# GNN hops: the weighted one-hot matrices of eight edge tiles are made by two VectorE instructions in place of eight

## The chip, the cores and the metric

The program runs on one core of one Trainium2 chip. The metric is the device time of one execution in microseconds (us), as the median of repeated runs. TensorE does the matrix products, VectorE and ScalarE elementwise work, GpSimd (POOL in the rows) issues the indexed gathers, SyncE plain DMAs. In rows PE is TensorE, PEld its weight loads, DVE is VectorE, ACT is ScalarE.

## The reference

Four layers follow one another on 6250 nodes with 256 features: a graph attention layer, a mixture of experts, a three-hop graph network, an LSTM that steps through the 6250 nodes. The change is in the third. There, with 100,000 edges:

```python
for i in range(3):
    msg = H[cols] * vals[:, None]
    Hn = jax.ops.segment_sum(msg, rows, num_segments=N)
    Hn = Hn @ Wn[i].T + bn[i]
    Hs = H @ Ws[i].T + bs[i]
    H = Hn + Hs
    if i != hop_num - 1:
        H = jax.nn.elu(H)
```

The kernel multiplies H by `Wn` first and puts the result into a table in DRAM (`hop_table`). What is left of a hop is: fetch one table row of 256 floats for each edge, scale it by the edge's weight, add it into the row of its target node. That is the function `propagate`.

## The kernel before

Edges are sorted by target and cut into tiles of 128, such that all targets of a tile lie in one block of 128 nodes. There are 832 tiles, padded ones at the end included. A hop takes them in rounds of U = 8, so 104 rounds, four rounds (NS = 4) to a loop body; three hops make 312 rounds and 2496 tiles. For a tile, a 128x128 matrix `S` has in row e the weight of edge e at the column of its target and zeros elsewhere; `S` transposed times the gathered rows `G` gives the sums of the tile, and these are added into block b of `agg` (in the last hop into `X`).

Each engine has a list of its own; semaphores alone tie them:

- **ScalarE** writes into a ring of four slots the row numbers of a round (`idx`, line 633; it waits until the gathers that used the slot four rounds ago have landed) and its targets and weights (`lw`, line 638).
- **GpSimd** issues eight indirect DMAs a round (line 657), 128 rows of 1 KB each, into slot r of `G`. It waits for `indexed`, and for `mm`: the products of four rounds earlier must be done.
- **TensorE** waits for the landing of the round's eight gathers (`got[r]`), then for each tile for `built` and `added`, and multiplies (line 671). Each float32 product is two MATMUL instructions in the trace.
- **VectorE** does two things in turn: `build` makes the `S` of one tile of the next round (line 680: compare `cols` with the tile's targets, times the weight), then the sum of one tile of this round is added (line 694: one operand from PSUM, one from SBUF) after a wait for that product. At the start of a round it loads eight block numbers (`TENSOR_LOAD`, line 608). `S` has two halves, used in turn.

A hop begins and ends with a barrier of all engines; between hops `hop_transform` makes the next table.

## Time and profile before

| | us |
|---|---|
| median of 3 runs | 17562.97 |
| lowest, highest | 17558.74, 17570.36 |
| span of the profiled execution | 17545.4 |
| a hop (4620 to 5685, 5798 to 6861, 6984 to 8048) | 1063 to 1065 each |
| the LSTM and what follows, from 8048 | 9497 |

The span is what the profiler sees of one execution on the core. A row of the timeline tells when an instruction, or a run of like ones, began, how long it took, and in brackets how long its engine had been idle before and what ended that. In grouped rows the number after the bar is the total busy time, then the mean of one in ns, then the idle time before them with what ended it. "issue" means that nothing in the profile was waited for.

### The profile page before, as it was taken

The numbers are of one execution on the slowest core, as the hardware profiler recorded it, in microseconds if no ns is written. First come the engines' busy times: TensorE is split into PE (matmuls) and PEld (weight loads), VectorE is DVE, ScalarE is ACT, GpSimd is POOL, SyncE is SP. The second block draws the span as 40 slices with busy tenths as digits, with TensorE's granted clock in tenths as the row PEclk, the third lists the DMA queues.
The fourth block names the chain that finished last, engine by engine and source line by source line (L and its number), as shares of the span: only waits on it lengthen the run. The fifth ranks groups of instructions, "written<-read, shape, count | busy, mean of one in ns | idle before, by whom it ended". The sixth has DMA issues, their size and how long they took to land. (4 is left out here: it accounts for less than half of the span.)

```text
span 17545.4 us, 683245 instructions
## 1 busy us (share of the span) xinstructions
PE 12730.7 (73%) x250869; PEld 10213.3 (58%) x250870; DVE 11697.3 (67%) x68713; ACT 5986.8 (34%) x41949; POOL 5631.1 (32%) x6174
## 2 busy tenths in 40 slices
PE   5247773399655656556888888888888888888887
PEld 3135552266444544445777777777777777777776
DVE  7368887322555454556777777777777777777777
ACT  0004442011100101003555555554555555555555
POOL 4778887666576575772000000000000000000000
PEclk6558886599877777775555555555555555555555
DMA  0102222111333333331000000000000000000000
GB/s 22 25 21 73 74 72 43 56 34 33 101 105 98 96 105 87 105 105 37 4 4 4 4 4 4 4 4 4 4 4 4 4 4 4 4 4 4 4 4 18
DMA packets 352412, 609.44 MB, mean 35 GB/s; under 512 B 157501, under 2 KB 232222, under 8 KB 348988
## 3 DMA queue, kind: packets, MB, share of 16 engines
q0 software_dynamic: 223104, 471.33, 10.4%
q1 hardware_dynamic: 126524, 100.27, 1.9%
q8 instruction: 1835, 30.06, 0.7%
q14 instruction: 949, 7.77, 0.1%
HBM read 508.72 MB, written 62.45 MB: 33 GB/s over the span
## 5 line engine op out<-in xcount | busy, mean ns | idle before, releaser
L2402 PE MATMUL lr_ZI<-ls_h,ls_V 128*128 128x1 f16 x150000 | 5006.8, 166 | 1669.7 <-DVE ls_h L2451 1412.8
L2402 PEld LDWEIGHTS lr_ZI<-ls_h,ls_V 128*128 128x128 f16 x150000 | 4487.3, 104 | 2677.0 <-DVE ls_h L2451 2640.4
L2419 ACT ACTIVATE ls_tg<-lr_ZI 128x2 f32<-128x2 f32 x12500 | 2150.0, 172 | 4626.5 <-PE lr_ZI L2402 4534.6
L2446 DVE TENSOR_TENSOR_SCAN lr_c<-ls_tg,ls_one_hc 128x2 f32<-128x2 f32 x12500 | 2118.1, 170 | 1441.0 <-ACT ls_tg L2419 1317.8
L2358 POOL COPY ls_HT<-ls_h 128x250 f32 x50 | 19.8, 395 | 9358.3 <-DVE ls_h L2456 9358.3
L2402 PE MATMUL lr_ZO<-ls_h,ls_V 128*128 128x1 f16 x75000 | 2865.0, 165 | 0.0
L671 PE MATMUL prop_sum<-prop_G,prop_S 128*128 128x256 f32 x4992 | 1830.4, 546 | 1369.9 <-DMA prop_G<-hop_table,prop_idx 1369.9
L657 POOL DMA_INDIRECT prop_G<-hop_table,prop_idx x2496 | 2368.3, 949 | 1057.3 <-issue 708.8
L2402 PEld LDWEIGHTS lr_ZO<-ls_h,ls_V 128*128 128x128 f16 x75000 | 2483.2, 104 | 0.0
L671 PEld LDWEIGHTS prop_sum<-prop_G,prop_S 128*128 128x128 f32 x4992 | 1403.9, 288 | 1796.3 <-issue 1486.1
L2451 DVE TENSOR_TENSOR ls_h<-ls_to 128x1 f16<-128x1 f32 x12500 | 2023.4, 162 | 479.1 <-ACT ls_to L2424 16.0
L2424 ACT ACTIVATE ls_to<-lr_c 128x1 f32<-128x1 f32 x12500 | 2102.5, 169 | 9.9 <-DVE lr_c L2446 1.0
L2422 ACT ACTIVATE ls_to<-lr_ZO 128x1 f32<-128x1 f32 x12500 | 2069.3, 171 | 0.0
L2455 DVE TENSOR_TENSOR_SCAN ls_h<-ls_to,ls_h 128x2 f16<-128x2 f32 x12500 | 1633.5, 162 | 25.7 <-issue 25.7
L694 DVE TENSOR_TENSOR gnn_agg<-gnn_agg,prop_sum 128x256 f32 x1664 | 694.9, 418 | 908.7 <-PE prop_sum L671 884.9
L2458 DVE TENSOR_TENSOR ls_one_hc<-ls_h,lr_c 128x1 f32<-128x1 f32 x6250 | 969.0, 155 | 220.0
L633 ACT CAST prop_idx<-gnn_SRT 128x8 int32 (+1 forms) x312 | 63.3, 203 | 2915.2 <-DMA prop_G<-hop_table,prop_idx 2903.7
L680 DVE TENSOR_SCALAR prop_S<-all_cols,prop_lw 128x128 f32<-128x128 f32 x2520 | 900.5, 358 | 165.6 <-issue 153.3
L2456 DVE TENSOR_TENSOR ls_h<-ls_to 128x2 f32<-128x2 f32 x6250 | 952.9, 152 | 7.2 <-issue 7.2
L2459 DVE TENSOR_TENSOR ls_one_hc<-ls_h,lr_c 128x1 f32<-128x1 f32 x6250 | 930.2, 149 | 0.0
L522 POOL DMA_INDIRECT sd_records<-sc_rec,sc_place x784 | 772.5, 985 | 440.7 <-issue 408.0
L1007 POOL DMA_INDIRECT all_X<-gat_table,gs_idx x832 | 825.3, 992 | 239.1 <-issue 239.1
(455 smaller groups left out, 13965.7 us busy)
## 6 DMA issues: line engine op xcount, KB each, us to landing
prop_G<-hop_table,prop_idx POOLq DMA_INDIRECT x2496, 2.7
mow_W<-in_L_ffn_W SPq DMA_DIRECT2D x16, 1024.0 KB, 10.8
moe_out<-me_Ys SPq DMA_DIRECT2D x108, 128.0 KB, 1.7
all_X<-gat_table,gs_idx POOLq DMA_INDIRECT x832, 2.8
hop_table<-ht_T SPq DMA_DIRECT2D x50, 256.0 KB, 2.1
sd_records<-sc_rec,sc_place POOLq DMA_INDIRECT x784
ss_records<-me_recs,me_places POOLq DMA_INDIRECT x540
gat_table<-gt_hs SPq DMA_DIRECT2D x50, 128.0 KB, 1.8
```

Of the source, the lines that this page charges most:

```text
L657: nc.gpsimd.indirect_dma_start(out=G[:, r, u, :], out_offset=None, in_=table[:, :], in_offset=bass.IndirectOffsetOnAxis(ap=idx[:, r, u:u + ...
L671: nc.tensor.matmul(ps[u][:, 0:D], S[:, r % 2, u, :], G[:, r, u, :], start=True, stop=True).then_inc(mm, 1)
L2402: mm = nc.tensor.matmul(place(hf, bank, col, 1), (V2 if part == "21" else V1)[:, q, ROWS.index(row), :], hx[:, prev, q, 1:2], start=False, ...
L2419: nc.scalar.activation(tg[:, s % 2, m, :], place(hf, m, col, 2), ACT.Tanh, scale=back).then_inc(gates[m], 1)
L2422: nc.scalar.activation(to[:, s % 2, m, 1:2], place(hf, KD + m, col, 1), ACT.Sigmoid, scale=back)
L2424: nc.scalar.activation(to[:, s % 2, m, 0:1], c[m][:, 1:2], ACT.Tanh, scale=0.5).then_inc(tanh_made[m], 1)
L2446: nc.vector.tensor_tensor_scan(c[m][:, 0:2], tg[:, e, m, :], one_hc[:, m, :], 1.0, ALU.mult, ALU.add).then_inc(cell[m], 1)
L2451: nc.vector.tensor_tensor(h1[:, r, m, 1:2], to[:, e, m, 1:2], to[:, e, m, 0:1], ALU.mult).then_inc(h1_made[m], 1)
L2455: nc.vector.tensor_tensor_scan(h2[:, r, m, :], to[:, e, m, :], h1[:, r, m, :], 1.0, ALU.mult, ALU.subtract).then_inc(h2_made[m], 1)
L2456: nc.vector.tensor_tensor(h[:, r, :], to[:, e, :, 1], to[:, e, :, 0], ALU.mult).then_inc(h_made, 1)
L2458: nc.vector.tensor_tensor(one_hc[:, 0, 1:2], h[:, r, 0:1], c[0][:, 1:2], ALU.mult)
L2459: nc.vector.tensor_tensor(one_hc[:, 1, 1:2], h[:, r, 1:2], c[1][:, 1:2], ALU.mult).then_inc(hc_made, 1)
```

## The change

`build` now makes all eight matrices of the next round at once with two instructions on 128x1024 elements. The first compares `cols`, repeated eight times, with `local`, each value repeated 128 times, and writes `same`; these three are bf16 tiles. The second multiplies `same` by `weight`, each value repeated 128 times, into the float32 half of `S`. Both have two operands in SBUF. The second waits for the first, and the first for the second of the round before (`compared` and program order). `build(n + 1)` stands behind the eight additions of round n; it stood between them tile by tile.

TensorE waits for `built` once a round, ahead of its first product. VectorE waits for `mm` ahead of every second addition, for two products at a time; it still waits for the addition before (`added`) each time. ScalarE makes `local` and `weight` by two copies in place of one. A bf16 copy of `cols` is made once a hop.

```diff
                 def prep(n, r, first=False):
                     if not first:
-                        act.wait_ge(built, U * (n - NS + 1))
-                    nc.scalar.copy(lw[:, r], SRT[:, bass.ds(n * U, U), 1:3]).then_inc(prepped, 1)
+                        act.wait_ge(built, n - NS + 1)
+                    nc.scalar.copy(local[:, r], SRT[:, bass.ds(n * U, U), 1])
+                    nc.scalar.copy(weight[:, r], SRT[:, bass.ds(n * U, U), 2]).then_inc(prepped, 1)
...
                         pe.wait_ge(got[r], before + i * (16 * U) + 16 * U)
+                        pe.wait_ge(built, n + 1)
                         for u in range(U):
-                            pe.wait_ge(built, n * U + u + 1)
                             pe.wait_ge(added, n * U + u + 1)
...
-                def build(n, r, u):
-                    if u == 0:
-                        dve.wait_ge(prepped, n + 1)
-                    nc.vector.tensor_scalar(S[:, r % 2, u, :], k.cols[:], lw[:, r, u, 0:1], lw[:, r, u, 1:2],
-                                            ALU.is_equal, ALU.mult).then_inc(built, 1)
-
-                for u in range(U):
-                    build(0, 0, u)
+                nc.vector.tensor_copy(cols[:], k.cols[:]).then_inc(compared, 1)
+
+                def build(n, r):
+                    dve.wait_ge(prepped, n + 1)
+                    dve.wait_ge(compared, n + 1)
+                    nc.vector.tensor_tensor(same[:], cols[:].unsqueeze(1).broadcast_to([P, U, P]),
+                                            local[:, r].unsqueeze(2).broadcast_to([P, U, P]), ALU.is_equal).then_inc(compared, 1)
+                    dve.wait_ge(compared, n + 2)
+                    nc.vector.tensor_tensor(S[:, r % 2], same[:], weight[:, r].unsqueeze(2).broadcast_to([P, U, P]),
+                                            ALU.mult).then_inc(built, 1)
+
+                build(0, 0)
                 with dve.Fori(0, QUADS) as i:
                     for r in range(NS):
                         n = NS * i + r
                         blocks = blocks_of(nc, mybir.EngineType.DVE, tile_block, n)
                         for u in range(U):
-                            build(n + 1, (r + 1) % NS, u)
                             b = blocks[u]
-                            dve.wait_ge(mm, NS * U + n * U + u + 1)
+                            if u % 2 == 0:
+                                dve.wait_ge(mm, NS * U + n * U + u + 2)
                             dve.wait_ge(added, U + n * U + u)
                             nc.vector.tensor_tensor(agg[:, bass.ds(b, 1), :], agg[:, bass.ds(b, 1), :],
                                                     ps[u][:, 0:D].unsqueeze(1), ALU.add).then_inc(added, 1)
+                        build(n + 1, (r + 1) % NS)
```

On VectorE, where one round of the first hop ends and the next begins, the kernel before has these rows (line, operation, output <- inputs, elements; `sum6` is the PSUM bank of tile 6):

```order
L694 TENSOR_TENSOR gnn_agg<-gnn_agg,prop0_sum6 128x256
L680 TENSOR_SCALAR prop0_S<-all_cols,prop0_lw 128x128
L692 REGISTER_ALU
L693 REGISTER_ALU
L694 ISA
L694 TENSOR_TENSOR gnn_agg<-gnn_agg,prop0_sum7 128x256
L608 ISA
L608 TENSOR_LOAD gnn_tbk
L679 REGISTER_ALU
L680 TENSOR_SCALAR prop0_S<-all_cols,prop0_lw 128x128
```

In this stretch one small instruction on `S` stands ahead of each addition.

On VectorE at the same place the changed kernel has:

```order
L700 TENSOR_TENSOR gnn_agg<-gnn_agg,prop0_sum6 128x256
L699 REGISTER_ALU
L700 ISA
L700 TENSOR_TENSOR gnn_agg<-gnn_agg,prop0_sum7 128x256
L684 TENSOR_TENSOR prop0_same<-prop0_cols,prop0_local 128x1024
L686 REGISTER_ALU
L687 TENSOR_TENSOR prop0_S<-prop0_same,prop0_weight 128x1024
L608 ISA
L608 TENSOR_LOAD gnn_tbk
L698 REGISTER_ALU
```

The additions now follow one another, and both large instructions stand between the last addition of a round and the load of the next block numbers.

## Rows read from the trace of the kernel before

**Rows 1.** Busy time by stage: one hop, and all behind the hops
```profile
core 0: us, PE busy (x) PEld busy (x) DVE busy (x) ACT busy (x) POOL busy (x), PEclk, DMA share, GB/s
...
4620.00:5685.00 1065.00, 610.69 (x1664) 468.19 (x1664) 559.10 (x1672) 38.16 (x210) 789.74 (x832) 0.73 0.38 102
...
8048.00:17545.00 9497.00, 7748.96 (x227648) 6678.26 (x227648) 7291.87 (x56538) 4782.49 (x37753) 20.86 (x54) 0.50 0.02 5
```

**Rows 2.** The page's costliest groups: the lines of the hops
```profile
L671 PE MATMUL prop_sum<-prop_G,prop_S 128*128 128x256 f32 x4992 | 1830.4, 546 | 1369.9 <-DMA prop_G<-hop_table,prop_idx 1369.9
L657 POOL DMA_INDIRECT prop_G<-hop_table,prop_idx x2496 | 2368.3, 949 | 1057.3 <-issue 708.8
...
L633 ACT CAST prop_idx<-gnn_SRT 128x8 int32 (+1 forms) x312 | 63.3, 203 | 2915.2 <-DMA prop_G<-hop_table,prop_idx 2903.7
L680 DVE TENSOR_SCALAR prop_S<-all_cols,prop_lw 128x128 f32<-128x128 f32 x2520 | 900.5, 358 | 165.6 <-issue 153.3
```

**Rows 3.** Line 657 alone: shortest, median and longest gather issue (ns)
```profile
L657 POOL DMA_INDIRECT prop_G<-hop_table,prop_idx x2496: 942/946/1032, 4622.2 to 8025.7; - x192
```

**Rows 4.** Timeline of a steady round, all engines
```profile
5503.58 0.95 POOL L657 DMA_INDIRECT prop_G<-hop_table,prop_idx  x1 [0.30 <-issue]
...
5504.83 0.94 POOL L657 DMA_INDIRECT prop_G<-hop_table,prop_idx  x1 [0.30 <-issue]
...
5506.60 5.38 PE L671 MATMUL prop_sum<-prop_G,prop_S 128*128 128x256 f32 x16 [4.67 <-DMA prop_G<-hop_table,prop_idx]
...
5507.90 0.42 DVE L694 TENSOR_TENSOR gnn_agg<-gnn_agg,prop_sum 128x256 f32 x1 [3.96 <-PE prop_sum L671]
5508.23 0.34 DVE L680 TENSOR_SCALAR prop_S<-all_cols,prop_lw 128x128 f32<-128x128 f32 x1
...
5508.75 0.42 DVE L694 TENSOR_TENSOR gnn_agg<-gnn_agg,prop_sum 128x256 f32 x1 [0.17 <-PE prop_sum L671]
...
5512.81 0.41 DVE L694 TENSOR_TENSOR gnn_agg<-gnn_agg,prop_sum 128x256 f32 x1
...
5516.58 5.38 PE L671 MATMUL prop_sum<-prop_G,prop_S 128*128 128x256 f32 x16 [4.61 <-DMA prop_G<-hop_table,prop_idx]
```

**Rows 5.** Timeline of the end of the first hop
```profile
5664.06 0.95 POOL L657 DMA_INDIRECT prop_G<-hop_table,prop_idx  x1 [0.30 <-issue]
...
5664.50 6.69 PE L671 MATMUL prop_sum<-prop_G,prop_S 128*128 128x256 f32 x16 [6.73 <-DMA prop_G<-hop_table,prop_idx]
...
5677.51 5.32 PE L671 MATMUL prop_sum<-prop_G,prop_S 128*128 128x256 f32 x16 [6.32 <-DMA prop_G<-hop_table,prop_idx]
...
5683.69 0.41 DVE L694 TENSOR_TENSOR gnn_agg<-gnn_agg,prop_sum 128x256 f32 x1
```

**Rows 6.** Groups of other VectorE instructions with two SBUF operands, by size
```profile
L1209 DVE TENSOR_TENSOR gs_M<-all_X,gs_M 128x512 f32<-128x512 f32 x208 | 142.1, 685 | 0.0
...
L247 DVE TENSOR_TENSOR sd_oh<-sdb_bins,sd_binrow 128x400 bf16<-128x400 f32 x138 | 77.6, 574 | 33.7 <-DVE sd_pos L343 27.1 <-PE sd_cnt L306 4.4 <-PEq L251 2.0
...
L1321 DVE TENSOR_TENSOR all_X<-all_X,gf_XL 128x12800 f32<-128x12800 f32 x1 | 13.5, 13493 | 0.0
```

**Rows 7.** Timeline of the first sort: GpSimd's DMA issues beside VectorE
```profile
299.65 0.57 DVE L339 TENSOR_TENSOR sd_ranks<-sd_rank,sd_run 128x400 f32<-128x400 f32 x1
...
299.98 0.96 POOL L522 DMA_INDIRECT sd_records<-sc_rec,sc_place  x1 [0.30 <-issue]
...
303.55 0.57 DVE L247 TENSOR_TENSOR sd_oh<-sdb_bins,sd_binrow 128x400 bf16<-128x400 f32 x1
303.76 1.20 POOL L522 DMA_INDIRECT sd_records<-sc_rec,sc_place  x1 [0.30 <-issue]
...
306.32 0.58 DVE L247 TENSOR_TENSOR sd_oh<-sdb_bins,sd_binrow 128x400 bf16<-128x400 f32 x1 [0.17 <-DVE sd_pos L343]
306.52 1.20 POOL L522 DMA_INDIRECT sd_records<-sc_rec,sc_place  x1 [0.31 <-issue]
```

**Rows 8.** Timeline in the first hop: a gather issue beside line 680
```profile
5519.68 0.34 DVE L680 TENSOR_SCALAR prop_S<-all_cols,prop_lw 128x128 f32<-128x128 f32 x1
5519.84 0.99 POOL L657 DMA_INDIRECT prop_G<-hop_table,prop_idx  x1 [0.30 <-issue]
```

More of the change, by code:

```diff
@@ L618, in propagate @@
         idx = ph.sb("idx", [P, NS, U], I32)
-        lw = ph.sb("lw", [P, NS, U, 2])
-        S = ph.sb("S", [P, 2, U, P])
+        cols = ph.sb("cols", [P, P], BF16)
+        local, weight = ph.sb("local", [P, NS, U], BF16), ph.sb("weight", [P, NS, U])
+        same, S = ph.sb("same", [P, U, P], BF16), ph.sb("S", [P, 2, U, P])
         ps = [ph.ps(f"sum{u}") for u in range(U)]
         indexed, prepped, built, mm, added = ph.sem("indexed"), ph.sem("prepped"), ph.sem("built"), ph.sem("mm"), ph.sem("added")
-        turns = ph.sem("turns")
+        turns, compared = ph.sem("turns"), ph.sem("compared")
         QUADS = ET // (NS * U)
```

## The prediction, made before the changed kernel ran

> **What bounds the kernel now.** I read the stages first, then the groups of the hops, then one round in order of time. The change touches only the three hops, 3 x 1065 us of a span of 17545.4 us; the 9497 us behind them run other lines [rows 1]. The span is 17.6 us under the median of 17562.97 us. That is time around the span which the change leaves alone, so what I add to the span I add to the median.
>
> In a hop no compute engine is busy for 60% of the time [rows 1]. GpSimd is the engine to look at: its 832 issues keep it busy for 790 us, and ahead of nearly each there are 0.30 us that wait for nothing [rows 1, 4]. One gather therefore costs 0.95 + 0.30 = 1.25 us, a round of eight 10.0 us, 104 rounds 1040 us of the 1065. In one round the reader should see this: the eighth gather starts at 5503.58, the ninth at 5504.83 with no other wait, TensorE starts at 5506.60, which is 3.0 us after the eighth, works 5.38 us, and sits idle for 4.61 us until the next landing, at 5516.58, one GpSimd period later [rows 4]. TensorE's 1370 us of idle time ahead of products are all put down to the gathers' landing [rows 2]. So the issue rate of GpSimd sets a hop. TensorE and VectorE have slack, and GpSimd is four rounds ahead of what it waits for.
>
> The end of a hop is different: the last gather starts at 5664.06, but its round's products start at 5677.51, 13.4 us later instead of 3.0 [rows 5]. The last four rounds (of padding mostly) land late, and there GpSimd is not what is waited for.
>
> **The change, part by part.** (1) Less VectorE work of the small kind: 2520 instructions of 358 ns, 900 us [rows 2]. They ran beside other work, so their removal gives nothing directly. New are two instructions of 1024 elements a round. No row has that size. VectorE instructions with two SBUF operands take 574 ns for 400 elements and 13493 ns for 12800 [rows 6], which is 1.04 ns an element; so 574 + 624 x 1.04 = 1.22 us each. The first is all bf16, and the lowest it could be is half the slope: 1.22 - 0.53 = 0.69 us. I take 1.22, since one operand repeats each element, as in line 247, which runs at the full slope (574 for 400 and 685 for 512 lie on the same line).
>
> (2) Fewer waits for products: each addition starts at least 0.23 us after its product; an addition behind another waits for its end (0.42 us) and, as in the row behind a TensorE release, some 0.17 us more or less [rows 4], so 0.56 us from one to the next. The last pair starts after the eighth product, which is done 5.4 to 6.7 us after TensorE's start [rows 4, 5]: the last addition starts 0.23 + 0.56 later, the compare 0.34 after that [5508.23 against 5507.90, rows 4]. The compare thus starts 6.5 to 7.8 us after TensorE began. The two instructions end 2.48 us later, at 9.0 to 10.3 us. The next landing is 10.0 us after the last. So the new matrices are ready in time in most rounds, and up to 0.3 us late in those where TensorE was slow. The cover of this edit is TensorE's idle 4.6 us; it is nearly used up. For the late rounds I add 8 us in all, between 0 and 60.
>
> (3) The part that counts, GpSimd's issue. Look at the first sort, where GpSimd issues indexed DMAs beside VectorE [rows 7]. Beside line 339, which reads PSUM and SBUF, an issue takes its usual 0.96 us. Where line 247, with both operands in SBUF, is running when the issue starts, it takes 1.20 us: it ends 0.84 us after VectorE (303.76 + 1.20 = 304.96 against 303.55 + 0.57 = 304.12), and in the second pair 0.82 us after. So the issue waits until about 0.12 us before the VectorE instruction's end, then needs its full 0.95 us. The small line 680 does the same on a small scale: 0.99 us at 5519.84 [rows 8]. The mean issue of the hops is 949 ns, the shortest 942 [rows 2, 3], so all such meetings together cost 2496 x 0.007 = 17 us today, and most of that goes away: I take -15 us.
>
> The new instructions both have two SBUF operands, and each is 1.22 us long. An issue that starts in the first 1.10 us of one is held to the end of these. Issues start every 1.25 us, so one meets the compare with a chance of 1.10 / 1.25 = 0.88 and loses 0.55 us on average: 0.48 us a round. The multiply starts about 0.04 us after the compare's end, by the wait between them. The next issue of a held one starts 1.25 us after its release, which is 1.13 us behind the compare's end; the multiply holds until 0.04 + 1.10 = 1.14 us. So a second loss is near zero, and I add 0.02 for the rounds where the compare was missed. Sum 0.50 us a round.
>
> Is the mean of an even spread right? Counted from the eighth gather's start, the compare starts at 3.0 + (6.5 to 7.8) = 9.5 to 10.8 us, and gathers start at 8.75, 10.0, 11.25. Compare starts of 9.5 give a loss of 0.6 us, of 9.95 about 1.0, of 10.05 to 10.15 none (both instructions fit between issues), of 10.8 about 0.65. The spread of TensorE's time covers one whole period, so I keep 0.50; the ends are 0.2 and 0.9.
>
> A held issue delays its landing, and so everything behind it: the loss is on the path in all but the last four rounds of a hop, where the landing is 10 us late anyway. 300 rounds x 0.50 = +150 us (60 to 270).
>
> The Trainium skill bears on this from both sides (SBUF — State Buffer, § Who interferes with whom). It says that a VectorE instruction with two SBUF inputs contends with a GpSimd instruction that reads SBUF; the 1.20 us rows agree. The same section says that `tensor_tensor` was not seen to stall DMAs issued by GpSimd, since writing descriptors needs the write side; by that alone the term would be 0, and the rows speak against it.
>
> (4) ScalarE's second copy: some 0.20 us a round like its neighbour at 203 ns, on an engine that waits 2915 us for landings [rows 2]; it hides there. What is queued behind it is the next round's `idx`, needed tens of us later: 0.
>
> (5) Ends of hops: a build of a 105th round stands last. It was spread between additions; now compare and multiply come after the last addition (start 5683.69 in the row, [rows 5]) and end 0.34 + 2.48 - 0.41 = 2.4 us after it, ahead of the barrier: 3 x 2.4 = +7 us. The first build hides under the first gathers.
>
> Sum: 150 - 15 + 8 + 0 + 7 = **+150 us**, so 17713 us, 0.85% slower.
>
> **Rivals.** *The instructions slip between the issues* (the other side: not slower). The phase settles where neither meets an issue, or these instructions do not hold an issue at all. For it: the window exists (compare at 10.05 to 10.15), and a delayed issue shifts the phase. Against it: TensorE's time varies by over 1 us from round to round (5.38 to 6.69), and the window is 0.1 wide. It decides when the loss is under 0.1 us a round. Time: 17563 - 15 + 7 + 8 = about 17563, at best 17548. That is the best there is: a gather cannot go below 942 ns, so nothing gives more than 17 us.
>
> *VectorE's round becomes the bound.* If chained additions or the wait between compare and multiply cost 0.2 us more each than I take, products, additions and build make a loop of 10.3 to 10.8 us, and TensorE no longer waits for landings but for `built`. GpSimd then runs ahead until its ring of four is full. For it: only 0 to 0.4 us of slack by (2). Against it: while issues are held the landing comes later too, which gives slack back. Time: (0.3 to 0.8) x 312, not in addition to but partly beside the holding, so +200 to +300: 17760 to 17860.
>
> *The compare runs at twice the rate.* Then it is 0.69 us and meets an issue with a chance of 0.57 / 1.25 = 0.46, for 0.28 us; the multiply, mostly alone, then 0.3 or less: 0.25 us a round, 75 us in all; with the rest 17638. The operand that repeats each element speaks against it. The Trainium skill (Vector Engine (DVE) Microarchitecture Reference, § Performance modes — why throughput varies by op and dtype) has such an operand at the single rate (with 2-byte operands, on trn2). No row here has bf16 operands of that form.
>
> **How the numbers follow.** Holding with an even spread 0.62, twice the rate 0.12, VectorE's loop as bound 0.16, slipping between 0.10. The predicted time is that of the first, 17713. The range leaves out half of the slipping case and the far end of the loop case: 17600 to 17850, that is +37 to +287; this also holds the bounds of 0.2 and 0.9 us a round up to the last few us. A difference of 0.2% is 35 us, about what a measurement of this kernel tells from no change. Slower by more: 0.89. Within: 0.10. Faster by more: 0.01, since nothing in the rows is worth over 17 us.
>
> **What would show it.** In the changed kernel's trace the mean of the gather issue should be near 0.949 + 0.50/8 = 1.01 us, with single ones up to 2.0 us, each ending 0.83 us after a compare or multiply; gaps of 0.30 us between issues as now; compare and multiply near 1.22 us; hops of about 1115 us; TensorE still released by landings in most rounds. The time behind the hops should be the same 9497 us. If issues stay at 0.95 us, part (3) is wrong. If TensorE is mostly released by line 687, the loop is the bound. If the compare takes 0.7 us, the rate was wrong.

## The result, and the profile of the changed kernel

The changed kernel takes 17635.21 us (median of 4 runs, 17632.45 to 17636.73), the kernel before 17560.86 us (4 runs, 17555.98 to 17570.36). The ratio is 1.0042, with an interval of 1.0029 to 1.0054: slower by 74 us. The direction was right and the time lies in the range, but the +150 us of the forecast is twice what came. The profiled execution has a span of 17635.0 us, 89.6 us over that of before. That is 15 us more than the difference of the medians. In every execution whose span and time are both on record the span is 1.7 to 1.8 us under the time, not 17.6 us as the prediction took it for the kernel before: by that, the profiled execution of before was some 16 us shorter than its median. The forecast adds to the median, so it does not hang on this. Of the 89.6 us, 5.9 us lie ahead of the hops, where the change touches nothing: the first gather starts at 4628.1 instead of 4622.2.

First the stages (the columns are those of [rows 1]): the first hop, and all behind the hops.

```profile
4628.00:5717.00 1089.00, 637.30 (x1664) 486.92 (x1664) 595.75 (x1041) 48.09 (x306) 815.52 (x832) 0.68 0.38 100
8138.00:17635.00 9497.00, 7748.94 (x227648) 6677.76 (x227648) 7318.70 (x56540) 4790.88 (x37753) 20.85 (x54) 0.50 0.02 5
```

Behind the hops nothing has moved: 9497 us, as in [rows 1]. From the first gather to the end of the last addition the three hops take 1088.6, 1089.9 and 1089.4 us; before they took 1062.0, 1062.5 and 1062.9. The sum of the differences is 80.5 us. Another 2.4 us each lie behind the last addition, and the 5.9 us ahead; together 93.6 us, against a difference of 89.6 us between the spans. The other 4 us are won back between the hops and behind them, and are not explained.

Now the costliest groups, then lines 659 and 684, 687 alone (shortest, median, longest in ns), and last what line 673's idle time ended with (us, times).

```profile
L673 PE MATMUL prop_sum<-prop_G,prop_S 128*128 128x256 f32 x4992 | 1912.1, 565 | 1367.1 <-DVE prop_S L687 1005.6
L659 POOL DMA_INDIRECT prop_G<-hop_table,prop_idx x2496 | 2448.1, 981 | 1061.9 <-issue 731.3
```

```profile
L659 POOL DMA_INDIRECT prop_G<-hop_table,prop_idx x2496: 942/946/1944, 4628.1 to 8116.0; - x192
```

```profile
L684 DVE TENSOR_TENSOR prop_same<-prop_cols,prop_local x315: 1218/1218/1226, 4627.5 to 8137.5; 128x1024 bf16<-128x1024 bf16 x158
```

```profile
L687 DVE TENSOR_TENSOR prop_S<-prop_same,prop_weight x315: 1224/1225/1226, 4628.7 to 8138.7; 128x1024 f32<-128x1024 bf16 x158
```

```profile
  DVE prop_S L687: 1005.6, 251
  DMA prop_G<-hop_table,prop_idx: 361.5, 61
```

Two signs of the prediction are there at once. The mean gather issue went from 949 ns [rows 2] to 981 ns, and the longest from 1032 ns [rows 3] to 1944 ns: issues are held. And TensorE, which in all 312 rounds before waited for a landing, now waits in 251 of them for line 687, the multiply: that is the sign named for VectorE's loop as the bound. TensorE's idle time before products is the same as before, 1367 against 1370 us. What has grown by 82 us is its own work, from 1830 [rows 2] to 1912 us: a mean of 565 ns a product instruction instead of 546, at a granted clock of 0.68 instead of 0.73 in the first hop. Which of the two, longer work or the new wait, is cause and which effect can't be read from this kernel alone. The two instructions are 1218 and 1225 ns long, as forecast.

The next view is the timeline of two rounds of the changed kernel, the columns as in [rows 4].

```profile
5501.13 1.22 DVE L684 TENSOR_TENSOR prop_same<-prop_cols,prop_local 128x1024 bf16<-128x1024 bf16 x1
5502.00 1.17 POOL L659 DMA_INDIRECT prop_G<-hop_table,prop_idx  x1 [0.30 <-issue]
5502.38 1.23 DVE L687 TENSOR_TENSOR prop_S<-prop_same,prop_weight 128x1024 f32<-128x1024 bf16 x1
5503.47 0.95 POOL L659 DMA_INDIRECT prop_G<-hop_table,prop_idx  x1 [0.30 <-issue]
...
5503.74 6.23 PE L673 MATMUL prop_sum<-prop_G,prop_S 128*128 128x256 f32 x16 [4.01 <-DVE prop_S L687]
...
5509.34 2.11 DVE L700 TENSOR_TENSOR gnn_agg<-gnn_agg,prop_sum 128x256 f32 x4 [0.61 <-PE prop_sum L673]
...
5511.38 1.22 DVE L684 TENSOR_TENSOR prop_same<-prop_cols,prop_local 128x1024 bf16<-128x1024 bf16 x1
5512.23 1.18 POOL L659 DMA_INDIRECT prop_G<-hop_table,prop_idx  x1 [0.30 <-issue]
5512.63 1.23 DVE L687 TENSOR_TENSOR prop_S<-prop_same,prop_weight 128x1024 f32<-128x1024 bf16 x1
5513.72 0.96 POOL L659 DMA_INDIRECT prop_G<-hop_table,prop_idx  x1 [0.30 <-issue]
...
5514.02 6.21 PE L673 MATMUL prop_sum<-prop_G,prop_S 128*128 128x256 f32 x16 [4.05 <-DVE prop_S L687]
```

Read one turn of the loop. TensorE starts at 5503.74 and works 6.23 us. The last four additions run as one chain, 5509.34 to 5511.45. The compare starts at 5511.38, which is 7.64 us after TensorE's start, the multiply at 5512.63, and its end at 5513.86 lets TensorE go at 5514.02: 10.28 us for this turn, 10.24 us in the mean of the rounds that the multiply releases. GpSimd's eight issues need 10.0 us.

Now the held issue. At 5502.00 it starts 0.87 us into the compare and takes 1.17 us: it ends at 5503.17, 0.82 us after the compare's end at 5502.35, just like the rows of the first sort [rows 7]. It loses 0.23 us. The next one starts at 5503.47, in the last 0.14 us of the multiply, and is not held. One round later, at 5512.23, the same thing happens at the same place. This repeats in most turns: GpSimd, which could go round in 10.0 us, is held by 0.23 us and so goes round in 10.24 us, with the loop. Over the three hops 303 issues started in the first 1.12 us of the compare (1.23 us in the mean, so 0.28 us lost each; the median one starts 0.86 us into it), and some 300 met the multiply (0.956 us, so 0.01 us lost). 292 of the 312 rounds have an issue of over 1.0 us.

### The profile page after: what moved, and what is told of

Same layout as the page of the kernel before. It is cut to its first block and busy times, and to the rows that moved or that the text cites. A ratio compares the mean times of both kernels' runs of the same rounds, so it can differ in the third digit from the quotient of the medians.

```text
span 17635.0 us, 678937 instructions
## 1 busy us (share of the span) xinstructions
PE 12819.6 (73%) x250869; PEld 10275.6 (58%) x250870; DVE 11843.8 (67%) x66826; ACT 6028.5 (34%) x42264; POOL 5706.3 (32%) x6174
## 5 line engine op out<-in xcount | busy, mean ns | idle before, releaser
L673 PE MATMUL prop_sum<-prop_G,prop_S 128*128 128x256 f32 x4992 | 1912.1, 565 | 1367.1 <-DVE prop_S L687 1005.6
L659 POOL DMA_INDIRECT prop_G<-hop_table,prop_idx x2496 | 2448.1, 981 | 1061.9 <-issue 731.3
L673 PEld LDWEIGHTS prop_sum<-prop_G,prop_S 128*128 128x128 f32 x4992 | 1460.7, 300 | 1818.4 <-issue 1490.8
L1075 PE MATMUL gs_O<-gs_M,gs_S 128*128 128x260 f32 x1664 | 667.8, 493 | 35.1 <-DVE gs_M L1216 20.8
```

What stands on the lines that cost most here:

```text
L659: nc.gpsimd.indirect_dma_start(out=G[:, r, u, :], out_offset=None, in_=table[:, :], in_offset=bass.IndirectOffsetOnAxis(ap=idx[:, r, u:u + ...
L673: nc.tensor.matmul(ps[u][:, 0:D], S[:, r % 2, u, :], G[:, r, u, :], start=True, stop=True).then_inc(mm, 1)
```

## The experiments

The first questions were two. **Theory H**: the holding of the gather issues by instructions with two SBUF operands is what costs. **Theory L**: the loop through VectorE (products, additions, compare, multiply, next products) is the bound, and costs by itself. The kernels take away the one, the other, or both. H and L are the names in the expectations: theory H has the holding alone set the round of 10.24 us, theory L the loop.

**Where the numbers come from.** The runs fell into five groups, each with its own runs of the kernel before. In one group (labels f_) that kernel took 17563.76 us, as in the first measurement. In the other four (e_, g_, h_, k_) the same kernel took 19584.95, 19441.42, 19449.55 and 19439.48 us. There is no trace of it in these; in those of the edited kernels the first gather started at 5918 to 6096 us instead of 4622, and the hops took 1230 to 1268 us, as gathers landed late: in e3_neither the median round of products began 26 us after its eighth gather's start, in f_neither, the same kernel, 3.0 us. One of these four ran on a chip under the same number as the f_ group, so the chip alone may not be the reason. Kernels are compared inside their group only. The f_ group tells the causes of the result; the others tell what the same edits do when something else is the bound.

**The group in which gathers land early.** The changed kernel once more:

> The changed kernel as it stands, beside the others of this group on one chip. If the gathers land as fast as in the first comparison (landing 3 us after the eighth issue, the hops of the kernel before 1062 us each), it is +74 us, with hops of 1089 us and a round of 10.24 us.

It took 17640.51 us, ratio 1.0044 (1.0024 to 1.0063), +77 us, with hops of 1088.6, 1089.8 and 1089.4 us, as expected.

**Holding without the loop.** The build of the next round's matrices goes ahead of this round's additions, so the loop is cut: compare and multiply run while TensorE works or waits. They still read two SBUF operands.

```diff
-                build(0, 0)
+                build(0, 0, True)
...
                         blocks = blocks_of(nc, mybir.EngineType.DVE, tile_block, n)
+                        build(n + 1, (r + 1) % NS)
                         for u in range(U):
...
-                        build(n + 1, (r + 1) % NS)
```

> The build ahead of the additions, two SBUF operands kept, so holding without the loop. Where the gathers land fast: theory L expects TensorE released by landings in nearly all rounds and a time that is not tied to 10.24 us a round (holding of 0 to 0.9 us a round, total 0 to +250 us); theory H expects round and total of the changed kernel, 10.24 us and about +74 us.

17699.17 us (two runs), ratio 1.0078 (1.0049 to 1.0107): +135 us. Cutting the loop made the kernel slower still. Theory H, which expected the changed kernel's +74 us, is refuted; theory L's range, 0 to +250 us, was too wide to fail. The page's rows of this kernel, and what ended TensorE's idle time:

```profile
L659 POOL DMA_INDIRECT prop_G<-hop_table,prop_idx x2496: 942/946/1999, 4625.8 to 8161.2; - x192
```

```profile
  DMA prop_G<-hop_table,prop_idx: 1273.7, 262
  DVE prop_S L689: 232.4, 50
```

TensorE is back at waiting for landings. (The 50 waits put down to line 689 are landings too: where a multiply ended just ahead of a round, that round started 2.9 to 3.0 us after its eighth gather, like the others.) The mean issue is 1002 ns. 288 issues met the compare, and took 1.425 us in the mean: 0.48 us lost each, 138 us in all or 0.44 us a round. This is the even spread of the prediction, with issues anywhere between 0.95 and 2.0 us, and nothing to lock them to one place. One of the long ones from its timeline:

```profile
4833.60 1.99 POOL L659 DMA_INDIRECT prop_G<-hop_table,prop_idx  x1 [0.30 <-issue]
```

**The loop without holding.** The order stays that of the change, but each of the two instructions gets one operand from PSUM: `cols` and a copy of `weight` lie in the bank that was the eighth sum's, and that sum takes the free half of the first bank. The waits of TensorE are moved accordingly. New is one copy of 0.16 us a round.

```diff
-        ps = [ph.ps(f"sum{u}") for u in range(U)]
+        banks = [ph.ps(f"sum{u}") for u in range(U)]
+        ps = [banks[u][:, 0:D] for u in range(U - 1)] + [banks[0][:, D:2 * D]]
+        cols, held = banks[U - 1][:, 0:P], banks[U - 1][:, D:D + 2 * U].rearrange("p (j u) -> p j u", j=2)
...
-                            pe.wait_ge(added, n * U + u + 1)
+                            pe.wait_ge(added, n * U + (U + 1 if u == U - 1 else U if u == 0 else u + 1))
...
-                    nc.vector.tensor_tensor(S[:, r % 2], same[:], weight[:, r].unsqueeze(2).broadcast_to([P, U, P]),
+                    nc.vector.tensor_tensor(S[:, r % 2], same[:], held[:, r % 2].unsqueeze(2).broadcast_to([P, U, P]),
...
+                def keep(n, r):
+                    dve.wait_ge(prepped, n + 1)
+                    nc.vector.tensor_copy(held[:, r % 2], weight[:, r]).then_inc(kept, 1)
```

> One operand of each large instruction in PSUM, build behind the additions, so the loop without holding. Where the gathers land fast: theory L expects a round of 10.2 us and +50 to +75 us; theory H a round of 10.0 us and a total within 15 us of the kernel before. Both expect issues of at most 0.95 us on average.

17600.27 us, ratio 1.0021 (1.0010 to 1.0032): +36.5 us. Theory L expected +50 to +75 us, theory H at most 15. Line 661 is its gather issue, line 690 its multiply. First its gather issue (shortest, median, longest), then the idle time of TensorE, then one turn, then the hop's end.

```profile
L661 POOL DMA_INDIRECT prop_G<-hop_table,prop_idx x2496: 940/946/963, 4625.0 to 8056.2; - x192
```

```profile
  DVE prop_S L690: 1223.6, 305
  DMA prop_G<-hop_table,prop_idx: 70.0, 7
```

```profile
5507.41 6.24 PE L675 MATMUL prop_sum<-prop_G,prop_S 128*128 128x256 f32 x16 [4.01 <-DVE prop_S L690]
...
5513.01 2.11 DVE L709 TENSOR_TENSOR gnn_agg<-gnn_agg,prop_sum 128x256 f32 x4 [0.61 <-PE prop_sum L675]
...
5515.04 1.22 DVE L686 TENSOR_TENSOR prop_same<-prop_sum,prop_local 128x1024 bf16<-128x1024 f32 x1
5515.28 0.95 POOL L661 DMA_INDIRECT prop_G<-hop_table,prop_idx  x1 [0.30 <-issue]
5516.29 1.22 DVE L690 TENSOR_TENSOR prop_S<-prop_same,prop_sum 128x1024 f32<-128x1024 bf16 x1
5516.53 0.95 POOL L661 DMA_INDIRECT prop_G<-hop_table,prop_idx  x1 [0.30 <-issue]
```

```profile
5666.91 0.95 POOL L661 DMA_INDIRECT prop_G<-hop_table,prop_idx  x1 [0.30 <-issue]
...
5671.24 6.24 PE L675 MATMUL prop_sum<-prop_G,prop_S 128*128 128x256 f32 x16 [4.00 <-DVE prop_S L690]
...
5691.72 6.24 PE L675 MATMUL prop_sum<-prop_G,prop_S 128*128 128x256 f32 x16 [4.00 <-DVE prop_S L690]
```

An issue that starts 0.24 us into either instruction keeps its 0.95 us; no issue of this kernel is over 963 ns (945 in the mean). So one PSUM operand takes the holding away, and the same instructions at the same length hold only with both operands in SBUF. TensorE waits for the multiply in 305 of 312 rounds and starts every 10.24 us; GpSimd goes round in 10.02 us and runs ahead. It ends its issues well before TensorE is through: three rounds of products begin behind the last issue, the last of them at 5691.72. The late landings at a hop's end [rows 5] then lie hidden under the loop: the last four rounds follow one another in 41.0 us here, in 52 to 53 us in the changed kernel. That is the larger part of why this kernel, with the same loop of 10.24 us, has shorter hops (1074.5, 1072.6, 1074.0 us) than the changed kernel.

**Neither.** Both edits together.

> Both edits: neither loop nor holding. Where the gathers land fast, both theories expect a round of 10.0 us, hops of 1060 us, total -15 to +5 us against the kernel before.

17553.37 us, ratio 0.9994 (0.9983 to 1.0005): -10 us, not to be told from the kernel before, and in the expected range of -15 to +5. Its gather issue and TensorE's idle time:

```profile
L661 POOL DMA_INDIRECT prop_G<-hop_table,prop_idx x2496 | 2358.6, 945 | 1059.0 <-issue 705.0
```

```profile
  DMA prop_G<-hop_table,prop_idx: 1084.2, 252
  DVE prop_S L692: 281.4, 60
```

The 60 waits for line 692 are landings as well, again 2.9 to 3.0 us after the eighth gather. So against this kernel, in one group: the loop alone costs 17600.27 - 17553.37 = 46.9 us, holding alone 17699.17 - 17553.37 = 145.8 us, and both 17640.51 - 17553.37 = 87.1 us. The costs do not add up to 193 us; with the loop, holding costs 40.2 us instead of 145.8. The hops alone, from first gather to last addition, say the same: 38.0, 139.9 and 84.6 us. Two things lie outside them. With the build behind the additions some 3 us more pass between a hop's last addition and the next hop, so about 7 us of the loop's 46.9 are the prediction's part (5). And the stage behind the hops, which no edit touches, took 9500 to 9514 us in the traces of this group; single costs are good to some 10 us.

Neither theory is the whole. L was right that the loop sets the round, and H alone is refuted twice; but beside the loop holding still costs 40 us.

**The groups in which gathers land late.** The same three kernels, and the change with one wait for each product again (`dve.wait_ge(mm, NS * U + n * U + u + 1)` ahead of each addition in place of the wait for each second one):

> The changed kernel, but the two large instructions for round n + 1 stand ahead of the additions of round n instead of behind them, so TensorE's next round no longer waits for them; GpSimd's issues can still be held by them. Theory L (the loop of products, additions, compare, multiply and back to TensorE takes 10.24 us and sets the round; the holding only takes up GpSimd's spare 0.24 us): TensorE is released by landings again in nearly all rounds, and the time differs from the changed kernel's +74 us, down if the new holding is under 0.24 us a round, up if it is over. Theory H (the holding alone sets GpSimd's round of 10.24 us, and the loop would be shorter but for it): same holding, same hop of 1089 us, total again about +74 us against the kernel before.

> The changed kernel, but one operand of each large instruction is in PSUM (cols, and a copy of the weights made at the start of a round while VectorE idles; the sum of tile 7 shares a bank with tile 0), so that neither has two SBUF operands. Both theories: issues of 0.95 us beside them, mean under 0.950. Theory L: the loop is as long as before, round 10.2 us, total +50 to +75 us. Theory H: round 10.0 us, total within 15 us of the kernel before.

> Both edits at once: operands in PSUM, and the build ahead of the additions. Theories L and H alike: round of 10.0 us set by GpSimd, hops of 1060 us, total -15 to +5 us against the kernel before. If it stays above +30 us, a third cause is at work (ScalarE's second copy, or the ends of hops).

> The changed kernel, but VectorE waits for each product by itself as the kernel before does, so that the last addition starts 0.23 us after its product and the loop is about 0.3 us shorter. Theory L: round about 10.0 to 10.1 us instead of 10.24, hop 1065 to 1075 us, total +20 to +45 us, unless the holding then grows. Theory H: no change, +74 us.

| kernel | us, before 19584.95 | ratio | mean issue, ns |
|---|---|---|---|
| e1_build_first | 19532.58 | 0.9978 (0.9966 to 0.9989) | 1017 |
| e2_no_holding | 19595.59 | 1.0005 (0.9995 to 1.0015) | 945 |
| e3_neither | 19585.61 | 1.0005 (0.9994 to 1.0015) | 945 |
| e4_wait_each | 19649.60 | 1.0043 (1.0026 to 1.0060) | 1008 |

Holding is as large in the issues as before (1008 to 1017 ns against 945 ns), but it does not decide the time: the kernel with the longest issues is the fastest. The timeline of e3_neither tells what does:

```profile
6315.26 3.23 DVE L712 TENSOR_TENSOR gnn_agg<-gnn_agg,prop_sum 128x256 f32 x6 [5.35 <-remote]
6315.98 0.94 POOL L661 DMA_INDIRECT prop_G<-hop_table,prop_idx  x1 [3.93 <-remote]
```

GpSimd stands for 3.93 us here, not for an issue that is held. Its one wait at this place beside that for the row numbers is for the products of four rounds earlier, so I take it that the ring of four is full and the rounds that it waits for are late themselves. It then has slack, and a held issue need not cost time. The expectations were worked out for early landings, and none of these times tests them: e2 is where H had it and e3 where both did, e1 and e4 where neither did. Nor was the changed kernel itself run in any group with late landings. So these runs neither support nor refute H or L for the result. Why the first is 52 us faster, and why the fourth is 65 us slower, is not explained.

Two more edits were made to the kernel before itself. In the one, the small builds stand behind the eight additions, and TensorE waits once a round for all eight: the order and waits of the change, with neither its instructions nor the paired waits.

```diff
                         pe.wait_ge(got[r], before + i * (16 * U) + 16 * U)
+                        pe.wait_ge(built, n * U + U)
                         for u in range(U):
-                            pe.wait_ge(built, n * U + u + 1)
...
                         for u in range(U):
-                            build(n + 1, (r + 1) % NS, u)
...
+                        for u in range(U):
+                            build(n + 1, (r + 1) % NS, u)
```

In the other, VectorE does one idle instruction of 1024 elements a round ahead of the additions, on a tile that nobody reads. It computes nothing that is needed. It is a multiply of two SBUF operands (in bf16 in g_, in float32 in h_ and k_) or, as the control, a reduction of one SBUF operand:

```diff
                         blocks = blocks_of(nc, mybir.EngineType.DVE, tile_block, n)
+                        nc.vector.tensor_tensor(J[:, 1], J[:, 0], J[:, 0], ALU.mult)
```

```diff
                         blocks = blocks_of(nc, mybir.EngineType.DVE, tile_block, n)
+                        nc.vector.reduce_sum(R[:], J[:, 0], AXX)
```

A third kernel is f_no_holding with one wait for each product.

> The kernel before with only the order and the wait of the change: its eight small matrix instructions of a round stand behind the eight additions, and TensorE waits once a round. The loop is then products, additions, eight small instructions (8 x 0.26 us from one start to the next plus 0.1) and back. Where gathers land fast, theory L (loop and holding each cost when it is alone, together the loop sets the pace): loop 10.24 - 2.48 + 2.2 = 9.95 us, landing first in most rounds, total 0 to +30 us. Theory of holding alone: 0 to -10 us.

> The kernel before plus one instruction a round that nobody waits for: a multiply of 128x1024 bf16 elements, both operands in SBUF, at the start of VectorE's round, where VectorE idles. All operands are bf16 and step by one, so it may run at twice the rate. The price of holding by itself, without the loop: if it takes 1.22 us, 0.45 us a round as where the build stands first (+135 us); if it takes 0.69 us, a meeting of 0.46 x 0.28 = 0.13 us a round, +40 us. If holding were nothing by itself: 0.

> Control for the run with the idle multiply: in its place a reduction over 128x1024 float32 elements, one SBUF operand, about 1.2 us. Issues beside it take 0.95 us, total within 10 us of the kernel before. If it costs as much as the multiply, VectorE's time and not the holding is the price.

> The kernel with one operand in PSUM and the build behind the additions, but each addition waits for its own product, as in the kernel before. If a fixed sum of durations makes the loop, the round shrinks by what the additions gain, 0 to 0.3 us, to 9.95 to 10.2 us, and the total falls from +37 to about 0 to +30 us. If TensorE's clock is part of the loop and falls into the same pattern each round, the round stays at 10.24 us and TensorE's share of it grows instead.

These too met late landings. The four were run again, with the multiply in float32, and two of them a third time; gathers landed late in those too:

> Only order and wait of the change, with the eight small instructions. Sum of durations 9.95 us or less, so that landings release TensorE: total 0 to +20 us. If the clock is in step with such a loop too: 10.24 us a round and about +35 us.

> The kernel before plus one multiply of 128x1024 float32 elements a round, both operands in SBUF, about 1.22 us, that nobody waits for. Holding alone is on the path when gathers land fast: an even spread gives 0.48 us a round, +145 us; the build that stands first gave +135 us with two such instructions. If the loss is tied to the wait for the build, it is 0.

> The same place and length, but a reduction with one SBUF operand (1220 ns): issues keep 0.95 us, total within 10 us of the kernel before.

> Operands in PSUM, build behind the additions, one wait for each product. Sum of durations: the round shrinks by what the additions gain (they start up to 0.3 us earlier), to 9.95 to 10.2 us, total 0 to +30 us. Clock in step: the round stays at 10.24 us, TensorE's work in a round grows from 6.24 us by what the additions gained, total +37 us as with waits in pairs.

> The kernel before plus one multiply of 128x1024 float32 elements a round, both operands in SBUF, that nobody waits for; gathers landing fast. Holding alone on the path: 0.4 to 0.5 us a round, total +120 to +150 us. If the loss needs the wait for the build: 0.

> Operands in PSUM, build behind the additions, one wait for each product; gathers landing fast. Sum of durations: the round shrinks from 10.24 to 9.95 to 10.2 us, total 0 to +30 us. Loop tied to when TensorE's clock rises: the round stays at 10.24 us and TensorE's work in it grows from 6.24 us, total +37 us.

| kernel | us | before | ratio |
|---|---|---|---|
| g_small_behind | 19439.45 | 19441.42 | 1.0000 (0.9988 to 1.0011) |
| h_small_behind | 19469.64 | 19449.55 | 1.0009 (0.9998 to 1.0021) |
| g_one_idle_two_sbuf | 19457.10 | 19441.42 | 1.0008 (0.9997 to 1.0019) |
| h_one_idle_two_sbuf | 19480.24 | 19449.55 | 1.0008 (0.9995 to 1.0021) |
| k_one_idle_two_sbuf | 19444.81 | 19439.48 | 1.0002 (0.9989 to 1.0015) |
| g_one_idle_reduce | 19473.42 | 19441.42 | 1.0014 (1.0003 to 1.0025) |
| h_one_idle_reduce | 19477.76 | 19449.55 | 1.0009 (0.9995 to 1.0023) |
| g_no_holding_wait_each | 19443.87 | 19441.42 | 1.0000 (0.9988 to 1.0011) |
| h_no_holding_wait_each | 19444.75 | 19449.55 | 1.0001 (0.9990 to 1.0013) |
| k_no_holding_wait_each | 19420.25 | 19439.48 | 0.9996 (0.9984 to 1.0007) |

In time they tell nothing apart. What was expected of them for early landings, +120 to +150 us for the idle float32 multiply or a loop shortened to +0 to +30 us by one wait for each product, stays untested. But their rows settle one point: which instruction holds an issue. First the groups of h_one_idle_two_sbuf, then those of h_one_idle_reduce, then two rows of the former's timeline.

```profile
L659 POOL DMA_INDIRECT prop_G<-hop_table,prop_idx x2496 | 2461.0, 986 | 1514.7 <-issue 730.6 <-PE prop_sum L673 362.4 <-ACT prop_idx L635 299.0
...
L694 DVE TENSOR_TENSOR prop_J<-prop_J 128x1024 f32<-128x1024 f32 x312 | 382.8, 1227 | 279.8 <-issue 236.5 <-PE prop_sum L673 21.1 <-remote 20.0
```

```profile
L659 POOL DMA_INDIRECT prop_G<-hop_table,prop_idx x2496 | 2364.7, 947 | 1649.5 <-issue 723.4 <-PE prop_sum L673 395.0 <-ACT prop_idx L635 311.8
...
L694 DVE TENSOR_REDUCE prop_R<-prop_J 128x1 f32<-128x1024 f32 x312 | 380.6, 1220 | 289.6 <-issue 260.2 <-PE prop_sum L673 17.9 <-remote 10.5
```

```profile
6305.67 1.23 DVE L694 TENSOR_TENSOR prop_J<-prop_J 128x1024 f32<-128x1024 f32 x1 [0.34 <-issue]
6306.30 1.41 POOL L659 DMA_INDIRECT prop_G<-hop_table,prop_idx  x1 [0.30 <-issue]
```

The two idle instructions are equally long, 1227 and 1220 ns, and stand at the same place. Beside the multiply the mean issue is 986 ns, beside the reduction 947 ns (and 949 ns in [rows 2], with neither). The issue at 6306.30 ends at 6307.71, 0.81 us after the multiply's end at 6306.90. So it isn't that VectorE is busy. With f_no_holding, where the same two instructions with one operand in PSUM hold nothing, what is left is that it reads two operands from SBUF.

## Why the prediction was right in sign and twice too large

The step that failed is in the sum: it adds part (3), holding on an even spread, at its full +150 us, next to a loop (part 2) put at +8. Measured, the loop costs 46.9 us (7 of them part 5), and holding beside it 40.2 us. With the 10 us that f_neither lies under the kernel before this makes the +77 us of f_after. That the time still fell into the range is in part luck: one term was too small by some 30 us, the other too large by 110.

**What bounds the kernel.** Right for the kernel before. That only GpSimd's issue rate sets a hop is no longer true after the change: two loops of nearly the same length stand there.

**Part (1), the instructions.** Right: 1218 and 1225 ns against 1.22 us, and the small instructions' removal gave nothing directly.

**Part (2), fewer waits: the step that failed first.** It put the compare at 6.5 to 7.8 us after TensorE's start, and the matrices at 9.0 to 10.3 us, so in time in most rounds, with +8 us for the rest. In the rows it is 7.64 us and 10.12 us, and TensorE starts at 10.28. The working was right in form, but I let TensorE's time spread over 5.4 to 6.7 us, while the rows now show 6.19 to 6.23 us in most rounds, with a mean of 6.13 us against 5.87 before. Also, the additions in pairs leave a chain of four at the end, 0.56 us apart, which falls behind the products: the compare starts 1.41 us after TensorE's last work (5511.38 against 5503.74 + 6.23), where the sum had 0.23 + 0.56 + 0.34 = 1.13. And the 0.16 us from the multiply's end to TensorE's start were left out. The loop is thus not 9.0 to 10.3 us but 10.24 us, steadily, on the wrong side of GpSimd's 10.0. All of it was needed: with TensorE at its former mean of 5.87 us the same chain comes to 5.87 + 1.41 + 2.48 + 0.16 = 9.92 us (an estimate from these rows). Why TensorE's rounds became longer is open: its granted clock was lower, 0.67 against 0.74 in the rows at the end, and no run changed the clock alone. Alone it costs 46.9 us (f_no_holding against f_neither), some 40 of them without part (5), where I had 8 in a range of 0 to 60. It costs less than 0.24 x 312 = 75 us, as the late landings at the hops' ends vanish under it.

**Part (3), holding: right in mechanism and alone in size, wrong in what it stands beside.** Alone it costs 145.8 us, where 0.50 us x 300 = 150 were forecast; the loss at the compare is 0.44 us a round, the forecast 0.48; at the multiply 0.01, the forecast 0.02. The paragraph on the even spread failed. It took the phase between GpSimd and the compare as spread over a whole period. It would be, were TensorE's start set by the landing alone. With the loop at 10.24 us, GpSimd drifts earlier against the compare by 0.24 us a round until an issue falls into it where it is held by just that much, 0.86 us after its start, and stays there: an issue that starts earlier in the compare is held longer, a later one less. The sizes fit: an issue that starts x into the compare is held by 1.10 - x, and a hold of 0.24 us a turn needs x = 0.86, which is the measured median. Holding then eats the slack that GpSimd has against the loop, 0.24 us a turn, and in such turns costs no more than it. What it adds beyond the loop, 40.2 us, can be read from the hops' ends: GpSimd is held back to the loop's pace, so it isn't ahead at the end, and the last rounds' late landings are paid again. Hops of 1089.3 us against 1073.7 in the mean are 15.6 us each, 46.7 in all, of the size of the 40.2. Some 11 us of each 15.6 are the last four rounds (52 to 53 us against 41.0); the rest is a mean turn of 10.28 us instead of 10.24, from turns in which more than the difference is lost.

```profile
5695.81 0.95 POOL L659 DMA_INDIRECT prop_G<-hop_table,prop_idx  x1 [0.30 <-issue]
...
5709.35 5.83 PE L673 MATMUL prop_sum<-prop_G,prop_S 128*128 128x256 f32 x16 [7.66 <-DMA prop_G<-hop_table,prop_idx]
...
5717.83 1.23 DVE L687 TENSOR_TENSOR prop_S<-prop_same,prop_weight 128x1024 f32<-128x1024 bf16 x1
5719.96 0.38 SPq L1881 DMA_DIRECT2D ht_Wn<-in_gnn_WnT  x1
```

This is the changed kernel's first hop's end: the last round's products start 13.5 us after the last issue, as in [rows 5]; in f_no_holding the same landings are hidden in the loop's rows above. That the phase locks is read from the timelines (the 1.17 and 1.18 us issues at the same place one turn apart, 303 meetings with a mean loss of 0.28 us and a median place of 0.86 us) and from the fact that cutting the loop brings the 0.48 us back. No run set the loop to another length to see the loss follow it, so that it follows is argued.

**The -15 us** for the small holds of before: f_neither, without any holding, has a mean issue of 945 ns in place of 949, which is 10 us over 2496 issues, and comes out 10 us below before. So 10 rather than 15, and the time alone can't tell it from nothing.

**Part (4), ScalarE:** right, both copies take 0.20 us and nothing waits for them. **Part (5), hop ends:** right; from the last addition to the next work it is 2.4 us more in each hop. Above, the multiply ends at 5719.06, and the first work behind the barrier starts at 5719.96.

**The rivals.** *VectorE's loop becomes the bound* had the right place and the wrong price. I gave it 10.3 to 10.8 us and put its cost on top of part of the holding, 17760 to 17860. The loop is at 10.24, and it takes away from the holding's price instead of adding to it. *Slipping between the issues* fell: 292 of 312 rounds have a held issue. But its thought, that a delayed issue shifts the phase, was the one that held: the phase settles, not in the window of no loss but where the loss makes up the difference of the periods. I had dismissed it by TensorE's spread. *Twice the rate* fell: 1218 ns, also with bf16 on both sides. The one instruction that ran faster, the idle bf16 multiply (694 ns), has no operand that repeats each element; it is another operation too, and no run changed the operand alone. The Trainium skill (Vector Engine (DVE) Microarchitecture Reference, § Performance modes — why throughput varies by op and dtype) was cited for that, and the rows of line 684 agree. The other statement, of the Trainium skill's SBUF — State Buffer, § Who interferes with whom, by which `tensor_tensor` was not seen to stall DMAs issued by GpSimd, doesn't hold here: 0.95 against up to 2.0 us. The rule beside it, that two SBUF inputs contend with a GpSimd instruction that reads SBUF and that at most one SBUF input or a reduction doesn't, agrees with the rows of the large instructions, the idle multiply and the reduction. The small line 680 holds an issue too, by up to 0.09 us [rows 3, 8]; no run here takes that apart.

## What to carry to other kernels

When an edit moves work into a loop that has slack by a few per cent of its period, compute the loop's new length from its own chain of rows before anything else, every small wait included: if it comes out above the period of what was the bound, costs on that other engine are no longer simply added. Here 40 of 146 us were left of them. Two periodic chains, of which the slower holds the faster at one point, can settle at a fixed phase; without the slower loop (f_build_first) the same holding spread evenly. And beside GpSimd's gather issues, where these are the bound, a VectorE instruction with two SBUF operands should be short, or have one operand in PSUM.

## What the runs showed of the hardware

- An indirect DMA issue on GpSimd takes 0.946 us. If it starts while a VectorE instruction with two SBUF operands runs, it ends 0.81 to 0.84 us after that instruction's end, for lengths from 0.57 us [rows 7] to 1.23 us, unless it starts in the last 0.12 us or so, when it keeps its length; the longest issue was 2.0 us. With one PSUM operand or in a reduction, the large VectorE instructions don't hold it (means of 945, and of 947 and 950 ns, the last two beside the small line 680 as in the 949 of before).
- A multiply of bf16 by bf16 with neighbouring elements takes 694 ns for 1024 elements, against 1218 ns for the bf16 compare, in which an operand repeats elements. It holds issues too, for a shorter time: mean 959 ns. The two groups of g_one_idle_two_sbuf:

```profile
L659 POOL DMA_INDIRECT prop_G<-hop_table,prop_idx x2496 | 2393.0, 959 | 1581.5 <-issue 722.7 <-PE prop_sum L673 368.4 <-ACT prop_idx L635 297.3
...
L694 DVE TENSOR_TENSOR prop_J<-prop_J 128x1024 bf16<-128x1024 bf16 x312 | 216.7, 694 | 288.7 <-issue 232.2 <-PE prop_sum L673 27.7 <-remote 23.3
```

- TensorE's granted clock was lower where VectorE's loop was the bound. The same stretch (5000 to 5600 us) of f_no_holding and f_neither, columns as in [rows 1]: TensorE works 6.24 us a round in the first, at a granted clock of 0.67, and 5.88 us in the mean in the second, at 0.74, with rounds that vary. It is idle for 4.0 us ahead of each round in the first, and for 3.2 to 4.8 us, 4.1 in the mean, in the second. Why the steadier round has the lower clock is not shown.

```profile
5000.00:5600.00 600.00, 363.80 (x936) 278.58 (x935) 342.51 (x646) 27.14 (x177) 452.81 (x479) 0.67 0.37 105
```

```profile
5000.00:5600.00 600.00, 353.15 (x964) 269.67 (x963) 357.79 (x661) 28.09 (x180) 453.56 (x482) 0.74 0.37 105
```

- The same kernel took 17564 us in one group of runs and 19440 to 19585 us in others, with gathers that land later. No run here tells why. An edit to the changed kernel (the build ahead of the additions) that lies 135 us above the kernel before in the one group lay 52 us below it in another.
- With one wait for each product the compare comes earlier: in a turn of k_no_holding_wait_each it starts 6.97 us after TensorE (6306.36 and 6313.33) instead of 7.63 us (5507.41 and 5515.04 in f_no_holding). Of the 0.66 us, 0.10 are TensorE's shorter work in that turn. What that is worth where gathers land early wasn't measured.

```profile
6306.36 6.14 PE L675 MATMUL prop_sum<-prop_G,prop_S 128*128 128x256 f32 x16 [7.74 <-DVE prop_S L690]
...
6313.33 1.22 DVE L686 TENSOR_TENSOR prop_same<-prop_sum,prop_local 128x1024 bf16<-128x1024 f32 x1
```
